# The mask of a cross-attention kernel: from two matmuls per half-batch to a ScalarE copy into PSUM

## The reference

```
a   = layer_norm(ctx)                      # 8 x 64 x 1024
Q   = x @ Wq.T;  K = a @ Wk.T;  V = a @ Wv.T
s   = einsum('bhtd,bhsd->bhts', Q, K) * 64 ** -0.5
s   = where(mask, s, -inf)                 # mask: 8 x 64, one bit for each context row
o   = softmax(s) @ V                       # heads joined again: 8192 x 1024
out = x + tanh(gate) * (o @ Wo.T)
```

## Time and profile before

| | us |
|---|---|
| median of 3 timed runs | 1564.25 |
| lowest and highest | 1563.99, 1564.56 |
| the profiled execution | 1560.93 |
| its span, first to last instruction | 1559.2 |
| TensorE busy | 1531.3 (98%) |
| VectorE busy | 1128.9 (72%) |
| ScalarE busy | 872.8 (56%) |
| GpSimd busy | 356.1 (23%) |

### The profile page before, as it was taken

The page is one execution under the profiler, slowest core; times in us unless marked ns, Lnnn a source line. Parts: engine busy times, 40 slices in busy tenths (PEclk is TensorE's granted clock), DMA queues, the critical chain, the costliest instruction groups (busy, mean ns, idle before and its releaser), DMA issues.

```text
span 1559.2 us, 20380 instructions
## 1 busy us (share of the span) xinstructions
PE 1531.3 (98%) x7104; PEld 1245.8 (80%) x7104; DVE 1128.9 (72%) x1356; ACT 872.8 (56%) x1874; POOL 356.1 (23%) x254
## 2 busy tenths in 40 slices
PE   7999899999999999999999999999999999999998
PEld 5666778888888888887887888888888888888887
DVE  6445888787878787879857777777777777777643
ACT  3556445454545454547766666666666666666521
POOL 5333000000000000001233344432344333444320
PEclk9999999999999999999999999999999999999999
DMA  7799765656565656556689344553445533445321
GB/s 251 222 364 392 275 215 178 210 202 222 178 220 187 211 182 216 190 188 184 202 292 294 115 136 142 157 157 114 125 125 168 169 123 120 123 145 167 109 93 69
DMA packets 225077, 289.77 MB, mean 186 GB/s; under 512 B 28240, under 2 KB 112336, under 8 KB 224976
## 3 DMA queue, kind: packets, MB, share of 16 engines
q1 hardware_dynamic: 224976, 288.48, 56.6%
HBM read 168.89 MB, written 116.39 MB: 183 GB/s over the span
## 4 chain that ended last, share of the span: by engine, by line
PE 90%; DMA 4%; DVE 3%; issue 1%; SPq 1%; ACT 0%; POOL 0%; DVEq 0%; ACTq 0%
PE banks L1036 28%; PE banks L1038 28%; PE banks L1037 28%; PE banks L1104 4%; PE banks L1065 3%; DMA wo_split_scratch<-wo_ring 1%; DMA xq<-x_t 1%; DMA m_scratch<-m_stage 1%; DVE parts L878 1%; DMA s_scratch<-c_out 1%; DVE a_sum L939 1%; DVE a_ring L872 1%; ACT a_ring L684 0%; PE banks L1160 0%; DMA c_out<-x 0%
## 5 line engine op out<-in xcount | busy, mean ns | idle before, releaser
L1036 PE MATMUL banks<-parts,a_ring 128*128 128x512 f32 x1792 | 711.6, 397 | 5.8 <-DVE a_ring L872 3.6
L1038 PE MATMUL banks<-parts,a_ring 128*128 128x512 f32 x1792 | 700.1, 391 | 0.0
L1037 PE MATMUL banks<-parts,a_ring 128*128 128x512 f32 x1792 | 698.9, 390 | 0.0
L1036 PEld LDWEIGHTS banks<-parts,a_ring 128*128 128x128 f32 x1792 | 336.9, 188 | 75.3 <-DVE a_ring L872 5.9
L1038 PEld LDWEIGHTS banks<-parts,a_ring 128*128 128x128 f32 x1792 | 336.8, 188 | 72.2
L1037 PEld LDWEIGHTS banks<-parts,a_ring 128*128 128x128 f32 x1792 | 337.4, 188 | 66.7
L961 DVE TENSOR_TENSOR c_out<-banks,c_out 128x1024 f32<-128x1024 f32 x160 | 195.5, 1222 | 147.9 <-PE banks L1038 142.6
L732 ACT ACTIVATE probs<-probs,neg_max 128x64 f32<-128x64 f32 x1024 | 259.1, 342 | 1.7 <-DVE neg_max L966 1.7
L684 ACT CAST a_ring<-a_sum 128x1024 fp32r<-128x1024 f32 x128 | 134.3, 1049 | 219.4 <-PE banks L1038 199.6
L597 POOL TENSOR_TENSOR probs<-probs,row_rec 128x512 f32<-128x512 f32 x128 | 134.5, 1051 | 479.7 <-DVE row_rec L975 479.7
L872 DVE TENSOR_TENSOR a_ring<-a_sum,a_ring 128x1024 fp32r<-128x1024 f32 x128 | 180.3, 1409 | 79.4 <-ACT a_ring L684 79.4
(11 more groups left out here) (75 smaller groups left out, 1354.4 us busy)
## 6 DMA issues: line engine op xcount, KB each, us to landing
xq<-x_t SPq DMA_DIRECT2D x32, 1024.0 KB, 6.8
s_scratch<-c_out SPq DMA_DIRECT2D x64, 512.0 KB, 3.1
probs<-s_scratch SPq DMA_DIRECT2D x128, 256.0 KB, 4.0
c_out<-x SPq DMA_DIRECT2D x64, 512.0 KB, 4.5
out<-c_out SPq DMA_DIRECT2D x64, 512.0 KB, 3.1
b_raw<-m_scratch SPq DMA_DIRECT2D x29, 1024.0 KB, 6.7
m_scratch<-m_stage SPq DMA_DIRECT2D x16, 1792.0 KB, 13.9
wo_split_scratch<-wo_ring SPq DMA_DIRECT2D x56, 256.0 KB, 5.7
```

The source lines that it names most:

```text
L1036: pe.matmul(to, wl, mh, start=first, stop=False, skip_group_check=joined)
L1037: pe.matmul(to, wh, ml, start=False, stop=False, skip_group_check=joined)
L1038: return pe.matmul(to, wh, mh, start=False, stop=last, skip_group_check=joined)
```

## The change

`mask_f`, in which the first stage computed the 0 or -2^100 of all 8 batches for all partitions, gets memory of its own (before it lay under `mask_mov`) and stays. `ones_row`, `mask_mov`, `make_mask` and the mask matmuls go. ScalarE's new `put_mask(n)` writes the row of the batch, repeated 16 times, into the two banks that P1 of round n will use (128 x 1024 elements, one instruction), and P1's first matmul doesn't open the sum: it adds to what stands there. The copies for rounds 0 and 1 stand before the score stage's first casts; that for round n > 1 in step 7(n-1) + 1, that is six steps ahead, and it waits for the counts that say that round n-2 has left these banks.

```diff
-        ones_row = sb("ones_row", [P, P], F32R)
-        mask_mov = sb("mask_mov", [P, NC, S], F32R)
-        mask_off = nc.sbuf_base - NC * S * 4
-        mask_f = nc.alloc_sbuf_tensor_at("mask_f", [P, B, S], F32, offset=mask_off)
+        mask_f = sb("mask_f", [P, B, S])
...
-            nc.gpsimd.memset(ones_row[:].bitcast(F32), 0.0).then_inc(rows_zeroed, 1)
...
-            pool.wait_ge(rows_zeroed, 1)
-            nc.gpsimd.memset(ones_row[0:1, :].bitcast(F32), 1.0).then_inc(rows_zeroed, 1)
...
+            def put_mask(n):
+                if n < 2:
+                    act.wait_ge(mask_step, 1)
+                    act.wait_ge(m_copied_a, 4 * GROUPS)
+                    act.wait_ge(m_copied_b, 4 * GROUPS)
+                else:
+                    act.wait_ge(copied, 4 * (n - 1))
+                    act.wait_ge(added, 3 * (n - 1))
+                src = mask_f[:, n // 2:n // 2 + 1, :].to_broadcast([P, 2 * NC, S])
+                to = banks[:, 2 * (n % 2):2 * (n % 2) + 2, :].rearrange("p g (h s) -> p (g h) s", s=S)
+                nc.scalar.copy(to, src).then_inc(mask_made, 1)
...
+            for n in range(2):
+                put_mask(n)
             for rnd, q in refills(-1):
                 split_b_hi(rnd, q)
             split_a_hi(0)
...
                 if s > 0:
                     copy_out((s - 1) // 7, (s - 1) % 7)
+                if s % 7 == 1 and s > 7 and s // 7 + 1 < ROUNDS:
+                    put_mask(s // 7 + 1)
                 for rnd, q in refills(s):
                     split_b_hi(rnd, q)
...
-            def make_mask(rnd):
-                wait(dve, item_done, 2 * (14 * (rnd - 1) + 8))
-                src = mask_u8[0:1, rnd:rnd + 1, :].to_broadcast([1, NC, S])
-                nc.vector.tensor_scalar(mask_mov[0:1], src, -1.0, BIG, ALU.add, ALU.mult).then_inc(mask_made, 1)
...
-            nc.vector.memset(mask_mov[:].bitcast(F32), 0.0).then_inc(rows_zeroed, 1)
-            dve.wait_ge(rows_zeroed, 3)
-            make_mask(0)
...
-                if s % 14 == 9 and s // 14 + 1 < B:
-                    make_mask(s // 14 + 1)
...
-                        pe.wait_ge(mask_made, rnd + 1)
+                        pe.wait_ge(mask_made, n + 1)
...
-                opens = k in ON_F[::2] or k == P1
-                if k == P1 and n < ROUNDS:
-                    pe.matmul(to, ones_row[:], mask_mov[:].rearrange("p h s -> p (h s)"), start=True, stop=False,
-                              skip_group_check=True)
-                    opens = False
+                opens = k in ON_F[::2] or (k == P1 and n >= ROUNDS)
```

More of the change, by code:

```diff
@@ L113, in xattn_kernel @@
         ident_made = sem("ident_made")
-        rows_zeroed = sem("rows_zeroed")
         mask_step = sem("mask_step")
```

## The result

The changed kernel took 1558.24 us (median of 11 runs, 1557.27 to 1561.04), the kernel before on the same chip 1564.26 (11 runs, 1562.80 to 1566.82). The ratio is 0.9965, 95% interval 0.9958 to 0.9973, which is 5.5 us less (4.2 to 6.6); the two medians themselves are 6.0 apart. Forecast were 1559.6 us and 4.66 less.

A forecast was written before the change was run, and what follows sets the result against it. TensorE, busy 98% of the span, was taken as the bound. 5.44 - 0.36 - 0.32 - 0.1 = 4.66 us off the profiled 1560.93 gives 1556.3; with 3.3 for the timed median 1559.6, range 1555.5 to 1563.0.

The forecast's parts named there:

- The matmuls kept: TensorE, rounds 1, 2, 4 to 8, 10 to 13, 15 (step = 7n + k): 0.454 us saved each, 5.44 us.
- The three pauses: TensorE before steps 24, 66, 102: pauses of 0.77, 1.01, 1.32 us hide the 0.45 us of mask matmuls before each.
- round 14: Step 102 hangs on ScalarE's cast at 728.11; with the new copy the round keeps nothing of its 0.45 us.
- Rivals 1 and 4: 1: all matmuls count, 7.26 us less, 1557.0, 12%. 4: full stretches set by something else, no change, 1564, 7% with unseen.
- The copy's price: ScalarE's 128x1024 copy into two PSUM banks: about 1.05 us long, 0.95 us in the queue, upper bound 2.3.
- Rival 3: Dear PSUM copy stalls steps 10, 24, 38, 52, 66, 80, 94, 102; gain gone at 1.87 us, at worst 1567.7; 9%.
- p - 0.8: Stall in us claimed at step 102 if each copy takes p us in ScalarE's queue.
- Copies with time to spare: Copies at the start, odd rounds' copies, and steps 8, 36, 50, 78, 92: cost 0; step 10's spare 1.12 becomes 0.57 us.
- The copy at step 99: ScalarE, before the exponentials, with 0.81 us idle behind: a 0.95 copy makes step 102 0.1 us later.
- The copies at steps 22 and 64: Ahead of refill casts with nothing to spare: steps 24 and 66 start 0.55 us later, net cost 0.36 and 0.32.
- the pause at steps 24 and 66: TensorE waits for VectorE's line 872, 0.77 and 1.01 us; forecast 1.79 and 2.02 after the change.
- The clock: Rival 2: longer pauses at steps 24, 66, 102 bring 1.2 GHz, 1.6 us each; 1564.4, or 1561.2 for one; 10%.

The follow-up runs named there:

- copies and matmuls: The kernel before, with all its mask matmuls, plus 16 ScalarE copies into the same banks at the changed kernel's places; 1565.15 us, ratio 1.0011.
- the last version: The changed kernel with copies moved away from the refill and the last output-weight piece of each 14 steps one step later; 1554.38 us, again 1554.23.
- the moved copies: The changed kernel with even rounds' copies a step earlier and round 15's in step 101, so none precedes a refill; alone 1557.91 us, ratio 0.9974.

## Why the prediction was right

**The matmuls kept: right.** Twelve rounds gave 0.45 each, 5.44 us.

**The three pauses as places where the matmuls are hidden: right.** They are there after the change, and round 14 kept nothing (102 goes from 1.32 to 1.78). Rivals 1 and 4 fell with that. Rival 1's number, 1557.0, lies near the measured time, but its mechanism would have left the pauses as long as before; they grow by 1.00 at step 24 with a store of the same length (7.09 and 7.10 us).

**The copy's price: right.** 1.015 us long, 0.95 in the queue. The nearest rows were the right ones: the cast SBUF to SBUF takes 1.049, the copy PSUM to SBUF 1.008. The Trainium skill says in "ScalarE: Activation LUTs", section "Step-by-step: what each stage is for", that ScalarE writes PSUM faster than SBUF; here that is 0.03 us against the cast, and the trace agrees with no more than that. Rival 3's break-even at 1.87 us was not reached; doubling the copy gave its stalls of 0.5 at five steps, but at step 102 only 0.57 instead of its p - 0.8 = 1.2.

**Copies with time to spare: right.** Cost 0 at the start and at step 8 and its like; 0.58 us were left instead of 0.57. What round 0 kept of its matmuls can't be read, since the start of step 3 moves by more from one execution to the next.

**The copy at step 99: 0 instead of 0.1.** The cast behind it now follows without a pause, and VectorE waits 0.18 us for it:

```profile
722.84 2.04 ACT L737 ACTIVATE probs<-probs,neg_max 128x64 f32<-128x64 f32 x8
724.76 1.05 ACT L677 CAST a_ring<-a_sum 128x1024 fp32r<-128x1024 f32 x1
...
725.85 1.68 DVE L876 TENSOR_TENSOR a_ring<-a_sum,a_ring 128x1024 fp32r<-128x1024 f32 x1 [0.18 <-ACT a_ring L677]
```

That wait is made up before step 102: its pause is 1.78 with the copy and 1.78 without it.

**The copies at steps 22 and 64: the mechanism right at 22, half right at 64.** From landing to step 24 it takes 0.54 us more, as forecast (0.55). But at step 28 only 0.20 more is left, not 0.36, and at step 70 also 0.20, not 0.32. At 22, VectorE's freedom from the mask's row shortens steps 24 to 28 by 0.34, where I had counted only the pause of 0.19; the step behind that pause is 0.11 shorter as well. The traces without copies show that 0.34 by itself: 31.86 after 32.20. At 64 step 66 comes only 0.18 later, and the wait of 0.23 at step 69 that was to go is still there (0.25). That the net came near the forecast there is luck. The copy does cost 0.53 at step 66 (10.83 after 10.30 with copies and matmuls), but something else moved: a wait of VectorE's addition (line 898, now 902). Before:

```profile
537.72 1.23 DVE L898 TENSOR_TENSOR b_raw<-b_raw 128x1024 f32<-128x1024 f32 x1 [0.46 <-DVE parts L878]
538.86 1.22 DVE L872 TENSOR_TENSOR a_ring<-a_sum,a_ring 128x1024 fp32r<-128x1024 f32 x1
```

and after:

```profile
537.29 1.22 DVE L876 TENSOR_TENSOR a_ring<-a_sum,a_ring 128x1024 fp32r<-128x1024 f32 x1
...
541.23 1.23 DVE L902 TENSOR_TENSOR b_raw<-b_raw 128x1024 f32<-128x1024 f32 x1 [0.45 <-DVE parts L882]
```

It stood ahead of the low part for step 66 and stands behind it now. In the four traces in which VectorE writes the mask's rows (the three of the kernel before, and copies and matmuls) it stands ahead, in the eight others behind, so it moves with VectorE's shorter list and not with the copies. What it waits for the trace doesn't say, and I didn't try it.

**The term that was mis-sized: the pause at steps 24 and 66 was taken as a constant.** The prediction carried the pauses 0.77 and 1.01 over as if the store ended at the same time after its issue. Their length hangs on that of one store, and one trace had shown one draw of it: in three executions of the kernel before the pauses were 0.77, 1.44 and 0.11 at step 24, and 1.01, 1.44 and 1.32 at step 66. The sum by parts, means of three traces each, from step 3 to the last step:

| part | forecast | measured |
|---|---|---|
| 12 rounds | 5.44 | 5.44 |
| copies at 22 and 64 | -0.36 - 0.32 | -0.20 - 0.20 |
| copy at 99 | -0.10 | 0 |
| store before 22 (mean 7.75 to 6.84) | 0 | +0.91 |
| store before 64 (mean 7.89 to 7.42) | 0 | +0.47 |
| from step 112 on (mean 741.85 to 742.12) | 0 | -0.27 |
| sum | 4.66 | 6.15 (1360.67 to 1354.53 is 6.14) |

The row from step 112 on is almost all in one place, step 113, whose length differs by 0.75 us between two executions of the changed kernel. Without the last three rows the change is worth 5.04 us; whether the two rows of the store are all of the execution is open (below). The three ratios give 5.5, 5.0 and 5.8.

**The clock: right that it holds, and that it was the risk.** Behind the pauses of 1.62 and 1.79 us idle no slow matmuls came; those of 2.19, 2.29 and 2.94 with each copy twice took it to the 1.2 GHz level. Length alone doesn't decide, though. In the third execution of the changed kernel, 2.90 us idle at the start of the score stage were followed by no slow matmul, and 2.34 us idle ahead of step 1 were:

```profile
170.11 0.50 PE L1035 MATMUL banks<-parts,a_ring 128*128 128x512 f32 x1 [2.90 <-DVE a_ring L876]
...
178.22 0.50 PE L1035 MATMUL banks<-parts,a_ring 128*128 128x512 f32 x1 [2.34 <-DVE a_ring L876]
...
179.67 0.63 PE L1037 MATMUL banks<-parts,a_ring 128*128 128x512 f32 x1
```

With a store of 7.7 us instead of 6.8 the changed kernel's pause at 24 would be 0.9 longer, which is 1.6 us idle (an estimate), still in the range seen to be harmless. With the longest store seen, 8.42, it would be 2.3 us idle, which is not: the margin was partly luck. The Trainium skill ("TensorE: Matmul & The Clock Gate", section "HAM oscillation — how this bites in real kernels") says that TensorE is set back when it idles long in a wait. From the score stage on, 15 of the 16 pauses of 2.19 us idle and more in the twelve traces agree; behind the shorter ones nothing of it is seen.

**Open.** Why the store took 6.6 to 7.1 us in all three traces of the changed kernel (and 6.73 with copies and matmuls), and 7.1 to 8.4 in the three of the kernel before. The ranges touch at 7.1, so with three traces each chance is not excluded. All twelve traces make it less comfortable: before step 22 the five with the copies at the changed kernel's places show 6.62 to 7.40 us, the seven others 7.09 to 8.42. Before step 64 the same split shows nothing (7.35 to 8.04 and 7.26 to 8.07). The copy of step 22 itself starts only after the store has landed, so if the copies shorten the store, these runs don't show how.

TensorE's waits say the same in a word (waited for, us in total, times, longest). The changed kernel:

```profile
PE banks L1035 <- DVE a_ring L876: 8.3, 6, 2.9
```

and the last version, in its second trace:

```profile
PE banks L1039 <- DVE a_ring L880: 5.6, 3, 2.9
```

The waits at steps 24 and 66 (0.66 and 1.22) are off the list, and most of what is left is the first, of 2.9 us, and step 102.

## What to carry to other kernels

Work taken off the busiest engine counts only where that engine doesn't wait for a chain which its own work doesn't start: go through its first instruction of every step, not through its share. Where such a chain hangs on a DMA, write its pause as issue + transfer + the rest. The rest repeats to 0.05 us, the transfer doesn't, and a single trace shows one draw; the cure is to take the wait out of the queue of the engine on the chain, here by one number in a table beside the moved copies, which together were worth 2.9 us, more than half of what the change itself was worth (5.0). The moved piece without the moved copies was not run.

## What the runs showed of the hardware

- The same store of 256 KB took 6.6 to 8.4 us from issue to landing in twelve traces, at the same place of the program, beside a load of 1 MB and a store of 512 KB.
- ScalarE writes two PSUM banks (128x1024, f32) in 1.015 us, from 64 columns repeated 16 times in the changed kernel and from 128 columns repeated 8 times with copies and matmuls alike. No row without a repetition was run; the cast SBUF to SBUF takes 1.049.
- TensorE's granted clock in the first 20 us was 1.00 in one trace of the kernel before and 0.95 in another. With other differences of the beginning, the start of step 3 lies between 188.15 and 191.93 us over all traces, more than half of what the change is worth; so a comparison of two traces should start behind it.
- Pauses of 2.19, 2.29 and 2.94 us idle cost TensorE 1.5 to 1.6 us more each in slow matmuls behind them. Those of 1.62 us, and of 1.79, cost nothing more, and once neither did one of 2.90.
- Behind a pause the second matmul starts 0.34 us after the first instead of 0.23, so a pause costs 0.1 us more than its start to start less the pitch.
